# Decoder block on one core: value rows made once and kept in DRAM, and P times them in 64-column halves

## The reference, cut to what matters

```python
x = layernorm(x + ttt(x))
q = rmsnorm((x @ Wq).reshape(B, 64, 16, 128), gq)      # 16 heads of 128
k = rmsnorm((ctx @ Wk).reshape(B, 64, 16, 128), gk)
v = (ctx @ Wv).reshape(B, 64, 16, 128)
attn = softmax(einsum('bqhd,bkhd->bhqk', q, k) / sqrt(128))
x = layernorm(x + einsum('bhqk,bkhd->bqhd', attn, v).reshape(B, 64, 2048) @ Wo)
x = layernorm(x + ffn(x))                              # int8-like rounding of x, h and the weights
```

## Time and profile before

| | us |
|---|---|
| median of 3 runs | 446.68 |
| runs | 445.23, 446.68, 454.71 |
| span of the profiled execution | 440.1 |

### The profile page before, as it was taken

The page is one execution under the profiler, slowest core; times in us unless marked ns, Lnnn a source line. Parts: engine busy times, 40 slices in busy tenths (PEclk is TensorE's granted clock), DMA queues, the critical chain, the costliest instruction groups (busy, mean ns, idle before and its releaser), DMA issues.

```text
span 440.1 us, 10666 instructions
## 1 busy us (share of the span) xinstructions
PE 362.4 (82%) x4506; PEld 212.4 (48%) x4506; DVE 266.0 (60%) x494; ACT 218.0 (50%) x584; POOL 120.9 (27%) x132
## 2 busy tenths in 40 slices
PE   3999979779977735596799999999999999996942
PEld 2445844435433212343465665755757557473621
DVE  1579945499996886504243384673946728367564
ACT  3035954545533333063646757468475584753320
POOL 3042891022040041103033332343223432233001
PEclk9999969988968969589899999999999999998975
DMA  8990000000323001901010010100100100000000
GB/s 260 240 365 11 1 4 5 3 4 3 81 75 101 2 0 35 211 7 48 0 41 11 1 48 12 44 6 13 49 12 25 25 14 0 12 3 0 12 0 25
DMA packets 17630, 19.93 MB, mean 45 GB/s; under 512 B 3360, under 2 KB 15024, under 8 KB 17328
## 3 DMA queue, kind: packets, MB, share of 16 engines
q1 hardware_dynamic: 17552, 19.24, 16.0%
q10 hardware_dynamic: 32, 0.02, 0.0%
HBM read 18.07 MB, written 1.18 MB: 44 GB/s over the span
## 4 chain that ended last, share of the span: by engine, by line
PE 50%; DVE 19%; ACT 13%; POOL 8%; issue 7%; DMA 1%; SPq 1%; POOLq 0%; DVEq 0%; ACTq 0%
PE ps L626 9%; PE ps L535 7%; PE ps L672 5%; PE ps L446 5%; PE ps L525 4%; PE ps L680 3%; PE ps L640 3%; PE ps L572 3%; POOL pr L1525 3%; POOL pr L1527 3%; PE ps L554 3%; PE ps L649 2%; DVE pr L1382 2%; DVE pr L1379 2%; DVE mx L1381 2%
## 5 line engine op out<-in xcount | busy, mean ns | idle before, releaser
L626 PE MATMUL ps<-xwq,x1t 128*128 128x512 f32 x128 | 65.0, 638 | 0.9 <-ACT x1t L997 0.9
L680 PE MATMUL ps<-mvo,cxp 128*128 128x256 f32 x256 | 58.4, 382 | 0.1
L680 PEld LDWEIGHTS ps<-mvo,cxp 128*128 128x128 f32 x256 | 47.6, 190 | 6.7 <-issue 0.4
L535 PE MATMUL ps<-ctxt,xwk 128*128 128x512 f32 x64 | 39.0, 716 | 2.4 <-issue 2.2
L975 ACT ACTIVATE qjunk<-ps 128x128 f32<-128x128 f32 x128 | 33.5, 280 | 9.9 <-PE ps L626 9.7
L896 ACT ACTIVATE ksq<-ps 128x512 f32<-128x512 f32 x32 | 19.0, 594 | 38.3 <-PE ps L525 28.2
L626 PEld LDWEIGHTS ps<-xwq,x1t 128*128 128x128 f32 x128 | 24.0, 202 | 27.5 <-issue 24.7
L985 ACT ACTIVATE qt<-ps 128x512 f32<-128x512 f32 x32 | 19.2, 601 | 23.4 <-PE ps L640 23.3
L525 PE MATMUL ps<-ksq,onehot 128*32 128x512 f32 x64 | 21.8, 680 | 9.2 <-ACT ksq L896 9.1
L672 PE MATMUL ps<-pt,ctx 64*128 64x512 f32 x64 | 28.0, 657 | 0.2 <-ACT cxp L1006 0.2
L975 ACT ACTIVATION_READ_ACCUMULATOR qjunk<-ps 128x1 f32 x128 | 27.1, 212 | 0.0
(11 more groups left out here) (212 smaller groups left out, 736.5 us busy)
## 6 DMA issues: line engine op xcount, KB each, us to landing
rkb<-kscale SPq DMA_DIRECT2D x16, 256.0 KB, 4.0
xn<-in_x_dram SPq DMA_DIRECT2D x4, 512.0 KB, 5.4
ctx<-in_ctx_dram SPq DMA_DIRECT2D x4, 512.0 KB, 8.7
xwo<-in_L_xattn_Wo_dram SPq DMA_DIRECT2D x1, 2048.0 KB, 14.2
xwq<-in_L_xattn_Wq_dram SPq DMA_DIRECT2D x4, 512.0 KB, 5.4
w1n<-in_L_ffn_w_gate_up_dram SPq DMA_DIRECT2D x1, 1408.0 KB, 8.9
xwv<-in_L_xattn_Wv_dram SPq DMA_DIRECT2D x1, 1024.0 KB, 11.0
xwk<-in_L_xattn_Wk_dram SPq DMA_DIRECT2D x1, 1024.0 KB, 16.5
```

What stands on the lines that cost most here:

```text
L535: mm(bank(6 + n % 2), xwk[:, h * XD:(h + 1) * XD], ctxt[:, half * BANK:(half + 1) * BANK], start=True, stop=True)\
L626: last = mm(bank(n % 2), x1t[:, (i % 2) * D + k * P:(i % 2) * D + (k + 1) * P], xwq[qn][:, k * BANK:(k + 1) * BANK], start=k == 0, stop=k ...
L680: last = mm(bank(6 + turn_of[("y", i, 0)] % 2, D), cxp[:, h * P:(h + 1) * P], mvo[:, h * D:(h + 1) * D], start=h == 0, stop=h == XH - 1)
```

## The change

Value rows are ctx of a batch entry times `mvo`: for each entry 64 tokens x 16 heads of 256, 1 MB. They are made once, in 64 units. A unit is two products of 64 columns by 512, one for the upper and one for the lower half of the partitions (`row_unit`), a copy by ScalarE and a store of 256 KB into `vrow` in DRAM. 44 units are mixed among the key units of the recurrence (`FILLS`, `FILL_PLACES`: 4, 8, 10 and 22 in the four chunks, 18 fills of the last behind its last own terms), 20 come in the main loop's steps -2, -1 and 0 (`LATE_PLACES`). SP stores them, and loads for each tile two blocks of 1 MB (`load_rows`).

In the main loop `context_sum`, its four copies and `attention_out` go; `attend` multiplies the transposed P by the rows: 8 head pairs x 2 entries, each 64 columns by 256, the two entries in the two halves of the same bank. The order of all queues is changed: exp, sum, both GpSimd products and the transposes of P of tile i-1 now come in step i, P times rows near its end, ahead of the scores of tile i. y's part stands ahead of z in VectorE's queue, and the sum over P behind the four reads of `gate_up` and x3's last step. exp stands ahead of the second query quarter on ScalarE. The second copy of ctx in SBUF is no longer loaded, nor is ctx loaded a second time. `key_scales(0)` moves from chunk 2 to chunk 3. The buffers that the rows need lie over `mvo`, `ctx2`, `cxp`, `us`, `sg`, `pr` and parts of `kt`.

```diff
-KEY_PLACES = [(2, 1, 2, 2, 1), (1, 2, 1, 1, 2, 1), (1, 2, 1, 1, 2, 1), (1, 2, 3, 2)]
+NVU = 4 * B
+NLATE = 20
+NVS = NVU - NLATE
+FILLS = ([u for n in range(XH) for u in (("key", n), ("row", n))]
+         + [u for n in range(12) for u in (("key", XH + n), ("row", XH + 2 * n), ("row", XH + 2 * n + 1))]
+         + [("row", n) for n in range(XH + 24, NVS)] + [("key", n) for n in range(NKU - 4, NKU)])
+FILL_PLACES = [(0, 2, 1, 2, 2, 1, 1), (1, 3, 2, 2, 5, 2, 1), (1, 3, 2, 2, 5, 2, 1), (1, 5, 0, 4, 5, 2, 18)]
+LATE_PLACES = {-2: 4, -1: 4, 0: 12}
+assert len(FILLS) == sum(map(sum, FILL_PLACES)) and sum(LATE_PLACES.values()) == NLATE
...
+        late_st = [us[:, 0:BANK], sg[:, 0:BANK], pr[:, XH * T:XH * T + BANK], pr[:, XH * T + BANK:2 * XH * T]]
+        rows_of = [(rvb0[:, :], rvb1[:, :]), (rva[:, 0:XH // 2 * D], rva[:, XH // 2 * D:XH * D])]
...
+        vrow = nc.dram_tensor("vrow", [B, P, XH // 2 * D], F32).ap()
...
+            def load_rows(t, b2):
+                b = 2 * t + b2
+                for n in range(4 * b, 4 * b + 4):
+                    if n < NVS:
+                        sp.wait_ge(*rows_stored(n))
+                    else:
+                        sp.wait_ge(*late_stored(n - NVS))
+                if t >= 2:
+                    sp.wait_ge(sem("turn_done"), turn_of[("y", t - 2, 0)] + 1)
+                sp.dma_start(rows_of[t % 2][b2], vrow[b]).then_inc(sem("ld_rows%d" % (t % 2)), 16)
...
-            roots_to_rows(0)
+            store_rows(0, 13)
             sp.wait_ge(sem("mg_done"), 2 * 2)
             load_xwq(0)
             load_x()
-            scales_out(0)
+            store_rows(13, 17)
+            roots_to_rows(0)
+            store_rows(17, 24)
             sp.wait_ge(sem("og_ready"), 2)
             load_xwq(1)
             load_xwq(2)
-            roots_to_rows(1)
+            store_rows(24, 36)
+            scales_out(0)
+            store_rows(36, NVS)
             sp.wait_ge(sem("mg_done"), 2 * NCH)
             load_xwq(3)
+            sp.wait_ge(*rows_stored(NVS - 1))
+            load_rows(0, 0)
+            sp.wait_ge(sem("key_done"), NKU)
+            load_rows(0, 1)
             sp.wait_ge(sem("k_summed"), NKU)
             scale_rows(0)
-            for half in range(2):
-                load(ctx2[half * T:(half + 1) * T, :].rearrange("p (b c) -> p b c", c=CD), ctx_in.rearrange("b s c -> s b c"), "ctx")
             scale_rows(1)
+            roots_to_rows(1)
+            for n in range(0, 8):
+                store_late(n)
             scales_out(1)
+            for n in range(8, NLATE):
+                store_late(n)
+            sp.wait_ge(sem("turn_done"), turn_of[("row", NLATE - 1, 0)] + 1)
+            for b2 in range(2):
+                load_rows(1, b2)
...
+            def row_unit(bk, n):
+                b, m = n // 4, n % 4
+                for odd in range(2):
+                    last = mm(ps[odd * T:(odd + 1) * T, bk * BANK:(bk + 1) * BANK], ctxt[:, b * T:(b + 1) * T],
+                              mvo[:, :].rearrange("p (h n) -> p h n", n=D)[:, 4 * m + odd:4 * m + odd + 3:2], start=True, stop=True)
+                return last
...
+                    fills(places[0])
                     state_products(c, 1)
-                keys(next(places))
+                fills(places[1])
                 if c < NCH - 1:
                     scores_ttt(c + 1, 0)
-                    keys(next(places))
+                    fills(places[2])
                     scores_ttt(c + 1, 1)
-                keys(next(places))
+                fills(places[3])
                 own_terms(c, 0)
-                keys(next(places))
+                fills(places[4] + places[5])
                 own_terms(c, 1)
-                for n in places:
-                    keys(n)
-            key_unit(next(units))
+                fills(places[6])
+            key_sum(NKU - 2)
+            key_sum(NKU - 1)
...
+            def late_row(n):
+                bk = open_turn("row", n)
+                turn_done(row_unit(bk, NVS + n))
+
+            def attend(i):
+                pe.wait_ge(sem("tp_evac"), tp_of[("pt", i, 1)] + 1)
+                pe.wait_ge(sem("ld_rows%d" % (i % 2)), 32 * (i // 2 + 1))
+                bk = open_turn("y", i)
+                for hp in range(XH // 2):
+                    for b2 in range(2):
+                        last = mm(ps[b2 * T:(b2 + 1) * T, bk * BANK:bk * BANK + D], pt[:, hp * P + b2 * T:hp * P + (b2 + 1) * T],
+                                  rows_of[i % 2][b2][:, hp * D:(hp + 1) * D], start=hp == 0, stop=hp == XH // 2 - 1)
+                turn_done(last)
...
                     h_transpose(i - 3)
                 if cur:
                     q_quarter(i, 1)
-                if prev:
-                    p_transpose(i - 1)
                 if last3:
                     ffn_down(i - 3)
-                if cur:
-                    q_quarter(i, 2)
-                    q_transpose(i, 0)
-                if prev:
-                    context_sum(i - 1, 0)
-                    context_sum(i - 1, 1)
-                if cur:
-                    q_quarter(i, 3)
-                    q_transpose(i, 1)
-                if nxt2:
-                    ttt_out(i + 2)
-                if prev:
-                    context_sum(i - 1, 2)
-                if cur:
-                    q_transpose(i, 2)
                 if last2:
                     x_transpose_q(i - 2)
-                if prev:
-                    context_sum(i - 1, 3)
-                if last2:
                     gate_up(i - 2, range(0, 2))
                 if cur:
-                    q_transpose(i, 3)
+                    q_transpose(i, 0)
+                    q_quarter(i, 2)
                 if last2:
                     gate_up(i - 2, range(2, 4))
                 if cur:
+                    q_transpose(i, 1)
+                    q_quarter(i, 3)
+                if nxt2:
+                    ttt_out(i + 2)
+                if cur:
+                    q_transpose(i, 2)
+                if prev:
+                    p_transpose(i - 1)
+                    attend(i - 1)
+                if cur:
+                    q_transpose(i, 3)
                     scores(i)
-                if prev:
-                    attention_out(i - 1, range(0, 8))
                 if nxt:
                     x1_transpose(i + 1)
-                if prev:
-                    attention_out(i - 1, range(8, XH))
+                for n in late_rows(i):
+                    late_row(n)
...
+                if kind == "row":
+                    act.wait_ge(sem("row_done"), n + 1)
+                    if n >= 4:
+                        act.wait_ge(*rows_stored(n - 4))
+                    A(vst[n % 4][:, :], bank(bk), ACT.Copy).then_inc(sem("row_staged"), 1)
...
+                fills(sum(places[1:4]))
                 output_root(2 * c - 1)
                 state_root(c, 1)
-                for n in places[2:-2]:
-                    keys(n)
+                fills(places[4])
                 gated_square(c - 1)
-                keys(places[-2])
+                fills(places[5])
                 output_root(2 * c)
-                keys(places[-1])
-            key_unit(next(units))
+                if c < NCH - 1:
+                    fills(places[6])
+            fills(3)
             output_root(2 * NCH - 1)
+            fills(5)
             output_root(2 * NCH)
+            fills(FILL_PLACES[NCH - 1][6] - 8)
+            key_roots(1)
...
                 if last3:
                     tp_out("hqt", i - 3)
+                if i >= 2 and prev:
+                    exp_p(i - 1)
                 if cur:
                     q_quarter(i, 1)
+                if last2:
+                    tp_out("xqt", i - 2)
+                if cur:
+                    tp_out("qt", i, 0)
+                if last2:
+                    silus(i - 2)
+                if cur:
+                    q_quarter(i, 2)
+                    tp_out("qt", i, 1)
+                    q_quarter(i, 3)
+                    tp_out("qt", i, 2)
                 if prev:
                     tp_out("pt", i - 1, 0)
                     tp_out("pt", i - 1, 1)
                 if cur:
-                    tp_out("qt", i, 0)
-                    q_quarter(i, 2)
-                if prev:
-                    context_out(i - 1, 0)
-                    context_out(i - 1, 1)
-                if cur:
-                    tp_out("qt", i, 1)
-                    q_quarter(i, 3)
-                if prev:
-                    context_out(i - 1, 2)
-                if cur:
-                    tp_out("qt", i, 2)
-                if last2:
-                    tp_out("xqt", i - 2)
-                if prev:
-                    context_out(i - 1, 3)
-                if cur:
                     tp_out("qt", i, 3)
-                if last2:
-                    silus(i - 2)
                 if nxt:
                     tp_out("x1t", i + 1)
-                if cur:
```

(33 more changed lines are left out.)

227 lines of the change are left out of this document (113 added, 114 removed).

## The result

The changed kernel takes 494.78 us, the median of 4 runs (490.51 to 496.27), where the kernel before takes 447.94 (445.23 to 454.71): a ratio of 1.112, with a 95% interval of 1.105 to 1.119. It is slower, as forecast, but by 47 us instead of 20, and it lies above the upper end of the range, 486. Some executions of one kernel take a few per cent longer, so all ratios here use the runs within 1.5% of the fastest of their kernel. The profiled execution has a span of 492.4 us, where the sum of the prediction came to 461.0. So 31.4 us are to be found between the steps of that sum and the trace.

What follows compares the result with a forecast made beforehand. TensorE bounds the old main-loop step; relieved, the step becomes a loop of latencies. In us: 440.1 + 4 + 13.9 + 11.6 - 0.2 (six steps) - 8.4 = 461.0, plus 6.6 to the median, 467.6, stated as 467; range 448 to 486.

Steps and rivals of the forecast that it cites:

- circle of latencies: Main-loop step, from z to the next z through the in-order queues: 27.0 us; as likeliest case 467 us, chance 0.56.
- From wo to z of tile 1: Stretch from wo's start with the 20 late rows: 59.7 us where it was 48.1, so +11.6.
- The half-rate spell: Main loop, gate pieces and a quarter after TensorE's 3 us wait: up to 1.7 us, in one step of four.
- The recurrence: Chunks 0 to 3 up to chunk 3's own terms: 1 to 10 us later, 4 taken.
- 3 earlier: Chunk 3 of the recurrence: better spread fills and no 9 us behind ScalarE's gated square make it 3 us earlier.
- The 18 fills: Behind chunk 3's own terms, 7 keys and 11 rows: 23 us where 9.1 us passed before, so +13.9.
- The tail: From z of tile 7 to the end: P times rows ends at z + 19 instead of z + 27.4, so -8.4 us.
- no price: SP's queue: stores moved between loads cost nothing, since what is behind each wait is due 10 us later.
- DMA stalls: Rival: stores lengthen some 18 issue stalls in the recurrence by 0.9 us each, giving 482 us; chance 0.15.
- Halves in turn: Rival: the paired 64-column products run one after the other on TensorE, giving over 500 us; chance 0.05.
- TensorE stays the bound: Rival for the main loop: P's circle is cut, a step falls to 22 us, total 435; chance 0.12.
- head fully hidden: Rival: no loss in chunks 1 to 3 and steps at 25.5 us, total 452; chance 0.12.

## Why the prediction was right and where it failed

**Direction and mechanism: right.** TensorE was relieved of 7 us a step, and the step became a circle of latencies, on average 29.8 us where it had been 27.4. The wait for `xqt`, the lateness of P behind `gate_up`, y ahead of z, and the 3.6 us for P times rows all stand in the trace where the prediction put them. The experiments confirm that it is the queue orders: 21 us come back when one of them is changed, 28 with both.

**From wo to z of tile 1: right.** 59.2 us measured, 59.7 forecast. The wait at the late rows was 3.4 instead of 2.5, and it is 3.1 with tiny stores, so the order of SP's queue makes it, which the forecast named, and exp held a late row for 1.8 instead of 1.6.

**The half-rate spell: right in place, wrong in frequency.** The step that failed says "I take it in one step of four: 27.4 a step", with a bound of 29. Measured against the circle for the step from 327.69:

| | forecast, from z | measured, from z |
|---|---|---|
| `gate_up` starts | 8.8 | 8.71 |
| second gate piece starts | 12.0 | 13.10 |
| sum over P starts | 13.85 | 14.91 |
| P's transposes | 17.5 | 19.01 |
| y starts | 22.95 | 24.63 |
| next z | 27.0 | 28.60 |

(The forecast of 12.0 is 12.4 less the 0.4 of the third piece.) The path to `gate_up` is within 0.1. Then 1.1 us go in half rate, and 0.5 by GpSimd's 2.46 us product. All six intervals begin like this or worse: from the first to the second gate piece they have 4.3 to 4.4 or 5.4 us in turn, where 3.2 was forecast, and the first four intervals are 28.1 or 28.6 and 29.6 or 29.8 in the same turn. In the last two the spell comes a second time, at P itself:

```profile
404.83 1.97 PE L731 MATMUL ps<-ident,pr 128*128 128x128 f32 x8 [2.04 <-POOL pr L1602]
407.48 5.60 PE L755 MATMUL ps<-rva,pt 128*64 128x256 f32 x32 [0.69 <-ACT pt L1063]
```

That interval takes 31.2. There is no `ttt_out` in these two steps, and TensorE waits 2.04 us for GpSimd instead of 1.69. Together +14.3. The prediction had both rows that show what one wait does (3.04 and 3.39 us idle, each with a slow stretch behind it), knew that a wait of 3 us would fall in every step, and still took one in four. No row gave that share. The clock's part is shown by three kernels that keep the circle and have steps without the spell: 26.96 and 26.97 with the quarter made twice, 26.98 in one step with tiny stores, 27.3 in four with short row products. The last two have the full 3.0 us wait, so one spell a step is what most executions show, not a law.

The Trainium skill (TensorE: Matmul & The Clock Gate, HAM oscillation) describes a loop in which the wait for a DMA in every tile brings the lower clock back each time. The wait here is for ScalarE, but every step of this execution agrees, with 1.36 instead of 0.77 for the first gate pieces; had this been used for the count, the forecast would have had six spells instead of one and a half.

**The recurrence: +4 taken, +11.7 measured.** 10 was the upper bound. By the state reads (VectorE's, at 80.40, 110.58 and 140.99 before and 85.81, 119.05 and 152.91 after) the loss is: 1.7 before the recurrence's first product, 3.7 in chunk 0, 3.1 in chunk 1, 3.4 in chunk 2, and 0.2 gained in chunk 3, sum 11.7. Chunks 1 and 2 lie within their 3 to 6 and 1 to 6. The terms that failed are three. Preparation was not in the sum at all: the first product of the recurrence is at 57.90 instead of 56.16. This can't be told from chance: in executions with this head it stands anywhere from 55.9 to 58.1, and in the second profile of the kernel before, the one with the quarter made twice, at 57.37. "Chunk 0 gains nothing and loses nothing": the same 11 fills and sums stand ahead of the state products, but 0.74 and 1.49 us of issue stall now fall among them, where before there was none, and 0.45 behind them. The rest of the 3.7 is not accounted for; the first fills are cold in both kernels (3.90 and 3.64 us). And "3 earlier" in chunk 3 was 0.2: the 9 us behind the gated square are gone, but TensorE's fills take their place, and 2.03 us of wait for the root's chain. The mechanism given for chunk 1, ScalarE's root, was right in kind: TensorE waits 1.16 us for the chain there, and the run with the earlier root has no such wait. It is under half of the chunk's 3.1 us; close behind comes TensorE's queue itself, which in 81 to 119 works 32.75 of 38 us. A fill often waits 0.26 to 0.31 for ScalarE's key copy to free its bank, as at 107.36.

**The 18 fills: 23 forecast, 29.2 measured.** Products were priced back to back, 0.96 to 0.98 each. Measured they are 1.01 for a row and 1.06 for a key, with 0.26 to 0.31 of wait for ScalarE's copy ahead of three of them. The wait of key 30 for the stores of the last rows was 2.88 us where 1.6 stood for this and the last root together (root 0.86), and behind it come the slow records 1.98, 1.84 and 1.87, some 2.5 us more. A wait and its cold stretch again.

**The tail: -8.4 forecast, -4.6 measured.** P times rows takes 5.32 instead of 3.6, and `gate_up` 2.81 for eight pieces, behind waits of 5.0 and 5.2 us. The same cause: in every run of the changed loop P times rows takes 5.1 us or more there.

**The stores:** "no price" holds in the recurrence; with tiny stores nothing is gained there, and 3 us between the own terms and wo, which the forecast had in part in its 1.6. "DMA stalls" fell. "Halves in turn" fell: 3.67 us. "TensorE stays the bound" and "head fully hidden" fell with the steps of 29.8 and the own terms at 181.3.

**From span to median.** The prediction added 6.6 us for what lies around the span. In every run here some 2 us lie outside it; the rest of the 6.6 was that the execution profiled before was a fast one. So of the 31.4 us miss in the span 4.2 are hidden in the final number, where 494.8 stands against 467.6; that much is luck.

Could the sum have been right? With what the spells and the slower GpSimd product do to the six steps (+14.3), one spell in the fills (+2.5) and the tail's (+3.8), it gives 481.6 in the span. Of the 10.8 left, 7.7 are the recurrence and the rest is the fills.

## What to carry to other kernels

When a change relieves the bound engine, lay out the circle that the in-order queues close, from one instruction to the same one a tile later; its longest wait names the queue order to change first. Here two changes of order gave back 28 us, where taking work off TensorE in every step, with the rows made for nothing, gave no gain at all (452.4 against 446.8). Where the rows of a kernel show slow records behind a wait of TensorE of some 3 us, price the wait plus those records in every iteration, 1 to 3 us here, and take the step without them as the lower bound: both occurred here, 24 to 1 in five kernels and 1 to 4 in a sixth. Work moved from a loop into an earlier stage is only cheap where that stage has idle time on the same engine; 63 us of row products, two thirds of them put where a chunk had 5.5 idle us, cost 42.

## What was unexpected of the hardware

- Adding 1.9 us of products to a step of TensorE made the six steps 10 us shorter in the profiled executions and the median 6.4 us: the wait fell from 3.01 to 1.54 us, and behind it the clock stayed at its upper level.
- Waits of equal length, 3.00 to 3.03 us at the same place of the loop, had a spell at the lower clock behind them in 24 of 25 cases in five kernels and in 1 of 5 in a sixth.
- Taking 15/16 of the columns of 128 products away made nothing faster that can be told: the granted clock fell from 1.00 to 0.71 and from 0.94 to 0.59 in the stretches where they stand, and wo came 6 us later.
- Products of 64 columns, two at once in the halves of a bank, run at the rate of full ones: 3.67 us for 8 pairs of 256, and 0.93 for a pair of 512. The Trainium skill (TensorEngine Tiling, Key Properties) says that a change of the tiling mode drains the engine. No idle shows at the changes, but a pair of 512 that stands alone among other forms takes 1.01 us from start to start instead of the 0.91 of four in a row, so a change may cost about 0.1.
- GpSimd's product of 128 x 1024 takes 2.46 us instead of 1.90 when VectorE's product with both inputs in SBUF is already running; where GpSimd starts first it keeps its 1.90, and an instruction of VectorE of 256 columns, begun behind it, takes 1.41 instead of 0.41.
